# Five SBUF-only operations of the retention, moved from VectorE to GpSimd

## The chip, the cores and the metric

One core of a Trainium2 chip runs the whole program in one launch. The metric is the device time of that launch in microseconds (us). The engines are named as the profile names them: PE is TensorE, ACT is ScalarE, DVE is VectorE, POOL is GpSimd, SP is SyncE.

## The reference

The input x is 4 sequences of 512 tokens with 128 channels. Four sublayers follow one another, each with a residual:

```python
x = x + attn_a(_layernorm(x))      # chunked linear attention
x = x + ffn(_layernorm(x))         # six layers, see below
x = x + attn_b(_layernorm(x))      # the retention
x = x + ffn(_layernorm(x))         # the same six layers again
```

The six layers of `ffn` hold a local windowed attention (16 heads of 64, queries and keys normalised to length 1 and rotated) and a gated feed-forward. The retention, which the change touches, is:

```python
def _L0_attn_b_ref(X, W_Q, W_K, W_V):
    Q = xpos(X @ W_Q)                      # x * cos_s + rot * sin_s
    K = xpos(X @ W_K, downscale=True)
    V = X @ W_V
    D = decay_mask(L, GAMMA)
    ret = jnp.einsum('bnd,bmd->bnm', Q, K) * D[None]
    return ret @ V
```

## The kernel before

Channels lie on the 128 partitions, tokens on the free axis; a sequence is a tile of 128x512. After a first stage (the linear attention) the program is a pipeline of steps in which each engine runs its own list of instructions and waits on semaphores. Step s does the attention part of one sequence in one layer (`cur`) and, beside it, finishes the attention and does the feed-forward part of the sequence of step s-1 (`prev`). There are 48 such units of work, and they run through the two passes over the six layers without a break, so there are steps 0 to 48. Within a step the 16 heads go in four quads of four heads, g or k = 0 to 3.

The order on each engine is written by hand, in the function `step` of that engine. A quad goes through these operations:

- PE `project` makes queries and keys of a quad in PSUM. ACT `evacuate` writes their squares to `u` (L1093) and a scaled copy to `ab` (L1094).
- POOL `add_squares(k)` (L1287, twice 128x512) adds the squares of the two halves. It releases `sq_sum[0]` and `sq_sum[1]`.
- PE `norms(k)` (L806) sums them over the channels, once behind each of the two semaphores; each of the two fp32 matmuls stands in the trace as two passes, each with its weight load (PEld). ACT `inverse_norms` (L1105, L1107) turns them to inverse lengths.
- DVE `turn(k)` (L1342, twice) and `add_keys` (L1347), POOL `add_queries(k)` (L1291): the rotation, unnormalised. DVE `normalise_keys` (L1352, L1356) and POOL `normalise_queries(k)` (L1296) scale by the inverse length.
- SP sends the queries and keys to other partitions, PE `scores` (L827), DVE `less_maximum` (L1362, L1365), ACT exponentials (L1111), DVE `sums` (L1371, L1373) and `turn_weights` (L1377, L1380), PE `values` (L848).

At the end of a step DVE runs `second_residual` (L1411), which finishes the previous sequence's layer in `zT` and releases `x2`. The counter of `x2` starts four ahead, so that a wait for `now.count(x2, -2)` in step s is a wait for the `second_residual` of step s-1.

The retention has no steps of its own. It rides in steps 22 to 26, spread between the operations of the quads: its first half on one sequence (`ret1`) in steps 22 to 25, its second half (`ret2`) one step later, in steps 23 to 26. Those five steps are written out; steps 1 to 21 and most of those after 26 are loops. The order on PE at the start of a retention step is:

```python
                            project(0, (2, 3))
                            values(-3)
                            ret_keys_by_queries()
                            norms(0)
                            project(1, (0, 1))
                            ret_out()
                            scores(-1)
                            ret_mean()
```

`ret_keys_by_queries` (L927) waits for the sums `k_sum` and `q_sum` of the step before. On DVE the retention operations are, in order: `ret_decay` (L1454), `ret_add` (L1423), `ret_residual` (L1460), `ret_centre` (L1428), `ret_centre2` (L1465), `ret_norm` (L1433), `ret_part` four times (L1441), `ret_norm2` (L1470), and `ret_sum` twice (L1447). `ret_keys_by_queries` of step s feeds `ret_decay`, which is the first thing on DVE in step s, followed by `turn(0)`. POOL had in these steps the operations of the quads alone; PE banks in PSUM are taken in a fixed cycle of three, so PE also waits until DVE or ACT has read a bank (`bank_free`).

Of the kernel before, what the change touches and what calls it, by code (L numbers as in the profile page):

```python
# [3 lines left out]
def build_hybrid(nc, x_rows, tabs, wa, wb, wf, out):  # L4
# [10 lines left out]
    ALU, ACT, AX = mybir.AluOpType, mybir.ActivationFunctionType, mybir.AxisListType  # L15
# [14 lines left out]
    with ctx:  # L30
# [31 lines left out]
        xT = sb("xT", [C, TOK])  # L62
        zT = sb("zT", [C, TOK])
# [379 lines left out]
        def order_of(ret1, ret2):  # L443

            if not ret1 and not ret2:
# [16 lines left out]
        q_sum, k_sum = per_quad("q_sum"), per_quad("k_sum")  # L462
# [11 lines left out]
        x2 = Signal("x2", 1, 1, 4)  # L474
# [4 lines left out]
        R = {n: Signal("r_" + n) for n in ("x", "mean", "xc", "sq", "var", "lnv", "rstd", "xn", "k", "kr", "qr", "v", "q", "v_sb", "k_part", "kr_part",  # L479
                                           "qr_part", "q_part", "k_sum", "q_sum", "s0", "s1", "s2", "out", "x2", "mean2", "xc2", "sq2", "var2",  # L480
                                           "lnv2", "rstd2", "z", "sum")}
# [16 lines left out]
        def stage_ffn():  # L498
            scope = ExitStack()
            with scope:  # L500
# [27 lines left out]
                rc, rsq, rc2, rsq2, part, rvals = (t(n, [C, N]) for n in ("rc", "rsq", "rc2", "rsq2", "part", "rvals"))  # L528
                rqk = t("rqk", [C, 2, N])
# [24 lines left out]
                def columns(b):  # L554
                    return slice(N * b, N * b + N)
# [24 lines left out]
                def halves(s):  # L580

                    of = lambda first: s - first if isinstance(s, int) and 0 <= s - first < B else None
                    return of(RET1), of(RET2)
# [695 lines left out]
                @block.gpsimd  # L1279
                def _(pool):  # L1280
                    def step(s, prev, cur):
                        now = Steps(pool, s + 1, POOL_USES)

                        def add_squares(k):
                            for i in range(2):
                                pool.wait_ge(sq_done.sem, now.count(sq_done, 4 * k + 2 * i + 1))
                                nc.gpsimd.tensor_tensor(u[:, 2 * i + 1, :], u[:, 2 * i, :], u[:, 2 * i + 1, :], ALU.add).then_inc(sq_sum[i].sem, 1)  # L1287

                        def add_queries(k):
                            pool.wait_ge(turned.sem, now.count(turned, k))  # L1290
                            nc.gpsimd.tensor_tensor(w[:, 0:2, :], w[:, 0:2, :], ab[:, k % 2, 0:2, :], ALU.add).then_inc(q_sum.sem, 1)  # L1291

                        def normalise_queries(k):
                            pool.wait_ge(q_sum.sem, now.count(q_sum, k))
                            pool.wait_ge(gain.sem, now.count(gain, k))
                            nc.gpsimd.tensor_tensor(ab[:, k % 2, 0:2, :], w[:, 0:2, :], rn[:, 0:1, :].broadcast_to([128, 2, N]), ALU.mult).then_inc(rope_q.sem, 1)  # L1296

                        if halves(s) != (None, None):
                            for k in range(3):
                                add_squares(k)  # L1300
                                add_queries(k)
                                normalise_queries(k)
                            add_queries(3)
                            add_squares(3)
                            normalise_queries(3)
                        elif cur:
                            add_squares(0)
                            add_queries(0)
                            normalise_queries(0)
                            add_squares(1)  # L1310
                            add_squares(2)
                            add_queries(1)
                            normalise_queries(1)
                            add_queries(2)
                            normalise_queries(2)
                            add_queries(3)
                            add_squares(3)
                            normalise_queries(3)

                    nc.gpsimd.memset(kb[:, :, :], 0.0).then_inc(zeroed, 1)  # L1320
                    steps_of(pool, step)

                @block.vector
                def _(dve):
                    def step(s, prev, cur):
                        now = Steps(dve, s + 1, DVE_USES)
# [90 lines left out]
                                    nc.vector.tensor_scalar_mul(dst[:, 0:C:2], src[:, 1:C:2], -1.0).then_inc(r_turned, 1)  # L1417
                                    nc.vector.tensor_copy(dst[:, 1:C:2], src[:, 0:C:2]).then_inc(r_turned, 1)

                        def ret_add():  # L1420
                            if ret1 is not None:
                                dve.wait_ge(x2.sem, now.count(x2, -2))
                                nc.vector.tensor_tensor(xT[:, columns(ret1)], xT[:, columns(ret1)], zT[:, columns(ret1)], ALU.add).then_inc(R["x"].sem, 1)  # L1423

                        def ret_centre():
                            if ret1 is not None:
                                dve.wait_ge(R["mean"].sem, ret1 + 1)
                                nc.vector.tensor_tensor(rc[:, :], xT[:, columns(ret1)], f, ALU.subtract).then_inc(R["xc"].sem, 1)  # L1428

                        def ret_norm():  # L1430
                            if ret1 is not None:
                                dve.wait_ge(R["rstd"].sem, ret1 + 1)
                                nc.vector.tensor_tensor(rc[:, :], rc[:, :], rsq[:, :], ALU.mult).then_inc(R["xn"].sem, 1)  # L1433

                        def ret_part(name, to, tab):
                            if ret1 is not None:
# [2 lines left out]

                                    dve.wait_ge(R["k_sum"].sem, ret1 + 1)  # L1440
                                nc.vector.tensor_tensor(to, bank("ret", 0, name), tab[:, :], ALU.mult).then_inc(R[name + "_part"].sem, 1)  # L1441

                        def ret_sum(i, name, one, two):
                            if ret1 is not None:
                                dve.wait_ge(R[one + "_part"].sem, ret1 + 1)
                                dve.wait_ge(R[two + "_part"].sem, ret1 + 1)
                                nc.vector.tensor_tensor(rqk[:, i, :], rqk[:, i, :], part[:, :], ALU.add).then_inc(R[name].sem, 1)  # L1447

                        def ret_decay():
                            if ret2 is not None:  # L1450
# [13 lines left out]
                                dve.wait_ge(R["mean2"].sem, ret2 + 1)  # L1464
                                nc.vector.tensor_tensor(rc2[:, :], xT[:, columns(ret2)], bank("ret", 0, "mean2"), ALU.subtract).then_inc(R["xc2"].sem, 1)  # L1465

                        def ret_norm2():
                            if ret2 is not None:
                                dve.wait_ge(R["rstd2"].sem, ret2 + 1)
                                nc.vector.tensor_tensor(zT[:, columns(ret2)], rc2[:, :], rsq2[:, :], ALU.mult).then_inc(R["z"].sem, 1)  # L1470

                        if ret1 is not None or ret2 is not None:
                            ret_decay()
                            turn(0)
                            ret_add()
                            add_keys(0)
                            ret_residual()
                            normalise_keys(0)
                            ret_centre()
                            less_maximum(-1)  # L1480
                            ret_centre2()
                            sums(-1)
                            turn_weights(-1)
                            turn(1)
                            ret_norm()
                            add_keys(1)
                            ret_turn_weights()
                            normalise_keys(1)
                            less_maximum(0)
                            turn(2)  # L1490
                            sums(0)
                            ret_part("k", rqk[:, 1, :], kcos)
                            residual()
                            ret_norm2()
                            turn_weights(0)
                            ret_part("kr", part[:, :], ksin)
                            centred()
                            add_keys(2)
                            normalise_keys(2)
                            ret_part("qr", rqk[:, 0, :], qsin)  # L1500
                            less_maximum(1)
                            turn(3)
                            normed()
                            sums(1)
                            evacuate_out()
                            ret_sum(1, "k_sum", "k", "kr")
                            ret_part("q", part[:, :], qcos)
                            add_keys(3)
                            turn_weights(1)
                            next_low()  # L1510
                            for j in range(3):
                                gated(j)
                            ret_sum(0, "q_sum", "q", "qr")
                            less_maximum(2)
                            normalise_keys(3)
                            sums(2)
                            turn_weights(2)
                            second_residual()
                            return
# [147 lines left out]
```

## Time and profile before

| what | value |
|---|---|
| median of 3 runs | 3166.32 us (3164.66 to 3171.8) |
| time of the profiled execution | 3168.24 us |
| its span in the profile | 3166.5 us |
| PE busy | 3005.7 us, 95% |
| DVE busy | 2880.3 us, 91% |
| ACT busy | 2272.7 us, 72% |
| POOL busy | 1807.9 us, 57% |
| chain that ended last | PE 40%, DVE 23%, ACT 19%, issue 10% |

The profiled execution took 1.7 us more than its span, which is what lies around it, and it is 1.9 us above the median. The busy shares are means over 49 steps of which only five are touched; what bounds those five has to be read from their own stretch. A busy time of DVE or POOL holds time in which the instruction had been issued and was waiting for the other of the two engines, as the rows below show.

### The profile page before, as it was taken

To read this page: it belongs to the slowest core of one execution; us is meant where nothing else is said; L and a number is where in the kernel's file an instruction comes from. 1 tells how busy PE (TensorE), PEld (TensorE's weight loads), DVE (VectorE), ACT (ScalarE), POOL (GpSimd) and SP (SyncE) were. 2 spreads that over 40 slices of the span, in tenths; PEclk is the share of its full clock that TensorE was granted. 3 is DMA by queue.
4 is the path that set the end of the run, shared out by engine and by line. 5 is a ranking of instruction groups with operands and counts; after the bars stand their busy time and mean duration, and the time that the engine had idled before them with its cause. 6 is when DMAs were issued, how large, how long until landed. Compare 5 with 4: busy or idle time off the path is not lost.

```text
span 3166.5 us, 93664 instructions
## 1 busy us (share of the span) xinstructions
PE 3005.7 (95%) x37896; PEld 1857.5 (59%) x37896; DVE 2880.3 (91%) x2671; ACT 2272.7 (72%) x3707; POOL 1807.9 (57%) x823
## 2 busy tenths in 40 slices
PE   8699999999999999999999999999999999999996
PEld 4356555665665566565566656556656555665653
DVE  5599999999999999999999999999999999999995
ACT  4467777777777777776667777777777777777774
POOL 8556565555656555555445565555656565555652
PEclk9799999999999999999999999999999999999998
DMA  9544544543544544454344354454445445445542
GB/s 317 169 110 116 144 115 107 145 122 98 156 117 101 144 117 117 118 154 113 84 133 106 91 152 117 107 133 124 112 121 141 112 122 133 112 118 134 125 112 59
DMA packets 254405, 398.04 MB, mean 126 GB/s; under 512 B 51148, under 2 KB 84872, under 8 KB 254280
## 3 DMA queue, kind: packets, MB, share of 16 engines
q1 hardware_dynamic: 254280, 396.41, 47.8%
q8 instruction: 74, 1.21, 0.2%
q14 instruction: 51, 0.42, 0.0%
HBM read 64.64 MB, written 19.92 MB: 27 GB/s over the span
## 4 chain that ended last, share of the span: by engine, by line
PE 40%; DVE 23%; ACT 19%; issue 10%; SPq 1%; POOL 1%; DMA 1%; DVEq 0%; ACTq 0%; POOLq 0%
PE ps L848 6%; PE ps L806 5%; PE ps L866 5%; PE ps L882 5%; PE ps L827 5%; PE ps L787 4%; ACT f_ab L1094 4%; DVE f_mx L1362 4%; DVE f_p L1365 3%; ACT f_u L1093 3%; DVE f_p L1377 3%; ACT ps L1105 3%; PE ps L789 3%; PE ps L788 3%; ACT f_p L1111 3%
## 5 line engine op out<-in xcount | busy, mean ns | idle before, releaser
L1291 POOL TENSOR_TENSOR f_w<-f_w,f_ab 128x1024 f32<-128x1024 f32 x192 | 549.2, 2861 | 526.9 <-DVE f_w L1342 526.9
L1296 POOL TENSOR_TENSOR f_ab<-f_w,f_rn 128x1024 f32<-128x1024 f32 x192 | 594.1, 3094 | 390.9 <-DVE f_rn L1352 380.9
L1287 POOL TENSOR_TENSOR f_u<-f_u 128x512 f32<-128x512 f32 x384 | 589.1, 1549 | 365.3 <-ACT f_u L1093 359.8
L1094 ACT ACTIVATE f_ab<-ps,f_pa 128x512 f32<-128x512 f32 x768 | 542.1, 706 | 1.2
L1093 ACT ACTIVATE f_u<-ps 128x512 f32<-128x512 f32 x768 | 467.1, 608 | 99.3 <-PE ps L789 93.6
L1342 DVE TENSOR_TENSOR f_w<-f_ab,f_tan 128x1024 f32<-128x1024 f32 x384 | 500.4, 1343 | 4.1 <-POOL f_ab L1296 2.3
L848 PEld LDWEIGHTS ps<-f_tb,f_v 128*64 128x64 f32 x6144 | 396.0, 137 | 102.1 <-issue 78.5
L848 PE MATMUL ps<-f_tb,f_v 128*64 128x160 f32 (+1 forms) x6144 | 442.2, 297 | 11.9 <-DMA f_tb<-f_pt 10.7
L1105 ACT ACTIVATE ps<-ps 128x512 f32<-128x512 f32 x384 | 204.7, 574 | 340.7 <-PE ps L806 340.2
L787 PE MATMUL ps<-f_xh,f_wh 128*128 128x512 f32 x768 | 380.7, 496 | 54.8 <-ACT f_ab L1094 44.5
L806 PE MATMUL ps<-f_u,f_ones 128*128 128x512 f32 x768 | 370.2, 604 | 6.9 <-POOL f_u L1287 4.1
L866 PE MATMUL ps<-f_ot,f_wout 128*128 128x512 f32 x768 | 365.7, 599 | 2.8 <-DVE zT L1411 2.7
L827 PEld LDWEIGHTS ps<-f_kb,f_qb 64*32 64x32 f32 x24576 | 268.6, 105 | 107.3 <-issue 104.1
L1371 DVE TENSOR_REDUCE f_rs<-f_p 128x16 f32<-128x1024 f32 x192 | 233.4, 1216 | 102.5 <-ACT f_p L1111 102.5
L1356 DVE TENSOR_TENSOR f_ab<-f_w,f_rn 128x1024 f32<-128x1024 f32 x192 | 314.9, 1640 | 6.6
L1111 ACT ACTIVATE f_p<-f_p 128x1024 f32<-128x1024 f32 x192 | 202.7, 1056 | 147.6 <-DVE f_p L1365 147.4
L827 PE MATMUL ps<-f_kb,f_qb 64*32 64x64 f32 x24576 | 303.5, 226 | 2.2 <-issue 2.2
L789 PE MATMUL ps<-f_xh,f_wl 128*128 128x512 f32 x768 | 304.6, 397 | 0.0
L788 PE MATMUL ps<-f_xl,f_wh 128*128 128x512 f32 x768 | 302.3, 394 | 0.0
L1377 DVE TENSOR_TENSOR f_p<-f_p,f_rs 128x1024 f32<-128x1024 f32 x192 | 290.7, 1514 | 1.9
L882 PE MATMUL ps<-f_fq,f_w 128*128 128x512 f32 (+1 forms) x576 | 274.1, 611 | 11.3 <-issue 3.8
L1380 DVE STREAM_TRANSPOSE f_pt<-f_p 128x1024 f32<-128x1024 f32 x192 | 239.1, 1246 | 20.9
(165 smaller groups left out, 4822.9 us busy)
## 6 DMA issues: line engine op xcount, KB each, us to landing
f_kb<-f_ab SPq DMA_DIRECT2D x384, 256.0 KB, 3.6
f_qb<-f_ab SPq DMA_DIRECT2D x384, 256.0 KB, 3.6
f_tb<-f_pt SPq DMA_DIRECT2D x1344, 64.0 KB
f_wh<-split_w SPq DMA_DIRECT2D x48, 384.0 KB, 4.4
f_wl<-split_w SPq DMA_DIRECT2D x48, 384.0 KB, 4.2
a_w_raw<-wqkv SPq DMA_DIRECT2D x24, 384.0 KB, 4.6
split_w<-a_w_hi SPq DMA_DIRECT2D x24, 384.0 KB, 4.6
split_w<-a_w_lo SPq DMA_DIRECT2D x24, 384.0 KB, 5.5
```

The costliest lines, as they stand in the source:

```text
L787: nc.tensor.matmul(bank("qk", g, i), wh[:, g, i, :], xh[:, :], start=True, stop=False)
L806: last = nc.tensor.matmul(ps[:, NO[i], :], ones[:, :], u[:, 2 * i + 1, :], start=True, stop=True)
L827: last = nc.tensor.matmul(ps[rows, SS[h], c0:c0 + 64], qb[dims, pair, w0:w0 + WIN], kb[dims, pair, w0:w0 + 2 * WIN], start=False, stop=Tru ...
L848: last = nc.tensor.matmul(ps[rows, NO[pair], 128 * tile:128 * tile + WIN * windows], v[:, tile, d0:d0 + 64], tb[:, 0:windows, 8 * (h % 2) ...
L866: last = nc.tensor.matmul(f, wout[:, 2 * g + i, :], ot[:, 2 * g + i, :], start=g + i == 0, stop=g + i == QUADS)
L882: nc.tensor.matmul(bank(kind, -1, j)[0:m], w1[:, first + 128 * j:first + 128 * j + m], fq[:, :], start=True, stop=True).then_inc(ready.sem, 1)
L1093: nc.scalar.activation(u[:, i, :], bank("qk", g, i), ACT.Square).then_inc(sq_done.sem, 1)
L1094: nc.scalar.activation(ab[:, g % 2, i, :], bank("qk", g, i), ACT.Identity, scale=pa[:, g, i:i + 1]).then_inc(qk_read.sem, 1)
L1287: nc.gpsimd.tensor_tensor(u[:, 2 * i + 1, :], u[:, 2 * i, :], u[:, 2 * i + 1, :], ALU.add).then_inc(sq_sum[i].sem, 1)
L1291: nc.gpsimd.tensor_tensor(w[:, 0:2, :], w[:, 0:2, :], ab[:, k % 2, 0:2, :], ALU.add).then_inc(q_sum.sem, 1)
L1296: nc.gpsimd.tensor_tensor(ab[:, k % 2, 0:2, :], w[:, 0:2, :], rn[:, 0:1, :].broadcast_to([128, 2, N]), ALU.mult).then_inc(rope_q.sem, 1)
L1342: nc.vector.tensor_tensor(w[:, a:4:2, :], ab[:, k % 2, 1 - a:4:2, :], tan2[:, a:a + 1, :].broadcast_to([128, 2, N]), ALU.mult).then_inc(tu ...
```

## The change

Five operations of the retention whose operands all lie in SBUF leave the list of DVE and join that of POOL: `ret_add`, `ret_norm`, `ret_norm2` and the two `ret_sum`. Each keeps its operands, its shape (128x512, fp32) and the semaphores that it waits for and releases. `ret_add` now stands ahead of `add_squares(0)`, `ret_norm` behind `add_squares(1)`, `ret_norm2` behind `add_squares(2)`, the first `ret_sum` behind `normalise_queries(2)` and the second at the end of the step, behind `normalise_queries(3)`. In steps 22 to 25 `ret_add`, `ret_norm` and both `ret_sum` run, in steps 23 to 26 `ret_norm2`: 20 instructions in all.

```diff
@@ POOL, step @@
                         now = Steps(pool, s + 1, POOL_USES)
+                        ret1, ret2 = halves(s)
...
+                        def ret_add():
+                            if ret1 is not None:
+                                pool.wait_ge(x2.sem, now.count(x2, -2))
+                                nc.gpsimd.tensor_tensor(xT[:, columns(ret1)], xT[:, columns(ret1)], zT[:, columns(ret1)], ALU.add).then_inc(R["x"].sem, 1)
+
+                        def ret_norm():
+                            if ret1 is not None:
+                                pool.wait_ge(R["rstd"].sem, ret1 + 1)
+                                nc.gpsimd.tensor_tensor(rc[:, :], rc[:, :], rsq[:, :], ALU.mult).then_inc(R["xn"].sem, 1)
+
+                        def ret_sum(i, name, one, two):
+                            if ret1 is not None:
+                                pool.wait_ge(R[one + "_part"].sem, ret1 + 1)
+                                pool.wait_ge(R[two + "_part"].sem, ret1 + 1)
+                                nc.gpsimd.tensor_tensor(rqk[:, i, :], rqk[:, i, :], part[:, :], ALU.add).then_inc(R[name].sem, 1)
+
+                        def ret_norm2():
+                            if ret2 is not None:
+                                pool.wait_ge(R["rstd2"].sem, ret2 + 1)
+                                nc.gpsimd.tensor_tensor(zT[:, columns(ret2)], rc2[:, :], rsq2[:, :], ALU.mult).then_inc(R["z"].sem, 1)
+
                         if halves(s) != (None, None):
-                            for k in range(3):
-                                add_squares(k)
-                                add_queries(k)
-                                normalise_queries(k)
+                            ret_add()
+                            add_squares(0)
+                            add_queries(0)
+                            normalise_queries(0)
+                            add_squares(1)
+                            ret_norm()
+                            add_queries(1)
+                            normalise_queries(1)
+                            add_squares(2)
+                            ret_norm2()
+                            add_queries(2)
+                            normalise_queries(2)
+                            ret_sum(1, "k_sum", "k", "kr")
                             add_queries(3)
                             add_squares(3)
                             normalise_queries(3)
+                            ret_sum(0, "q_sum", "q", "qr")
@@ DVE, step: the four functions of the same names are taken out, and from its order @@
                             ret_decay()
                             turn(0)
-                            ret_add()
                             add_keys(0)
...
                             turn(1)
-                            ret_norm()
                             add_keys(1)
...
                             residual()
-                            ret_norm2()
                             turn_weights(0)
...
                             evacuate_out()
-                            ret_sum(1, "k_sum", "k", "kr")
                             ret_part("q", part[:, :], qcos)
...
                             for j in range(3):
                                 gated(j)
-                            ret_sum(0, "q_sum", "q", "qr")
                             less_maximum(2)
```

The order of POOL at the border of two retention steps, from quad 3 of step 23 into step 24. Before:

```order
123 L1291 TENSOR_TENSOR f_w<-f_w,f_ab 128x1024 [waits turned]
124 L1287 TENSOR_TENSOR f_u<-f_u 128x512 [waits sq_done] x2
125 L1296 TENSOR_TENSOR f_ab<-f_w,f_rn 128x1024 [waits gain,q_sum]
126 L1287 TENSOR_TENSOR f_u<-f_u 128x512 [waits sq_done] x2
127 L1291 TENSOR_TENSOR f_w<-f_w,f_ab 128x1024 [waits turned]
```

and in the changed kernel, where line 1302 is `ret_add`, 1313 is `ret_sum`, and 1288, 1292 and 1297 are what 1287, 1291 and 1296 were:

```order
131 L1292 TENSOR_TENSOR f_w<-f_w,f_ab 128x1024 [waits turned]
132 L1288 TENSOR_TENSOR f_u<-f_u 128x512 [waits sq_done] x2
133 L1297 TENSOR_TENSOR f_ab<-f_w,f_rn 128x1024 [waits gain,q_sum]
134 L1313 TENSOR_TENSOR f_rqk<-f_rqk,f_part 128x512 [waits r_qr_part,r_q_part]
135 L1302 TENSOR_TENSOR xT<-xT,zT 128x512 [waits x2]
136 L1288 TENSOR_TENSOR f_u<-f_u 128x512 [waits sq_done] x2
137 L1292 TENSOR_TENSOR f_w<-f_w,f_ab 128x1024 [waits turned]
```

Between `normalise_queries(3)` of one step and the squares of quad 0 of the next, where nothing stood, there are now two instructions, and the second waits for `x2`.

The order of DVE at the same border, before, from `second_residual` (L1411) and `ret_decay` (L1454) on:

```order
308 L1411 SCALAR_TENSOR_TENSOR zT<-ps,f_pf,f_x 128x512 [waits f_w2]
309 L1454 TENSOR_TENSOR f_hid<-ps,f_decay 128x512 [waits r_s0]
310 L1454 TENSOR_TENSOR f_hid<-ps,f_decay 128x384 [waits r_s1]
311 L1454 TENSOR_TENSOR f_hid<-ps,f_decay 128x128
312 L1454 TENSOR_TENSOR f_hid<-ps,f_decay 128x256 [waits r_s2]
313 L1342 TENSOR_TENSOR f_w<-f_ab,f_tan 128x2x512 [waits qk_read,rope_k,rope_q]
314 L1342 TENSOR_TENSOR f_w<-f_ab,f_tan 128x2x512
315 L1423 TENSOR_TENSOR xT<-xT,zT 128x512 [waits x2]
316 L1347 TENSOR_TENSOR f_w<-f_w,f_ab 128x1024 [waits turned]
317 L1460 TENSOR_TENSOR xT<-xT,ps 128x512 [waits r_out,r_x]
318 L1352 SCALAR_TENSOR_TENSOR f_rn<-ps,f_cos 128x1024 [waits n_inv]
```

and in the changed kernel, where 1443, 1470, 1374, 1379, 1476 and 1384 are the lines of 1411, 1454, 1342, 1347, 1460 and 1352:

```order
299 L1443 SCALAR_TENSOR_TENSOR zT<-ps,f_pf,f_x 128x512 [waits f_w2]
300 L1470 TENSOR_TENSOR f_hid<-ps,f_decay 128x512 [waits r_s0]
301 L1470 TENSOR_TENSOR f_hid<-ps,f_decay 128x384 [waits r_s1]
302 L1470 TENSOR_TENSOR f_hid<-ps,f_decay 128x128
303 L1470 TENSOR_TENSOR f_hid<-ps,f_decay 128x256 [waits r_s2]
304 L1374 TENSOR_TENSOR f_w<-f_ab,f_tan 128x2x512 [waits qk_read,rope_k,rope_q]
305 L1374 TENSOR_TENSOR f_w<-f_ab,f_tan 128x2x512
306 L1379 TENSOR_TENSOR f_w<-f_w,f_ab 128x1024 [waits turned]
307 L1476 TENSOR_TENSOR xT<-xT,ps 128x512 [waits r_out,r_x]
308 L1384 SCALAR_TENSOR_TENSOR f_rn<-ps,f_cos 128x1024 [waits n_inv]
```

The only row that left this place is `ret_add`; `turn(0)` is now followed by `add_keys(0)` directly.

## Rows read from the trace of the kernel before

**Rows 1.** Busy time by stretch: step 21, steps 22 and 23; column heads first
```profile
core 0: us, PE busy (x) PEld busy (x) DVE busy (x) ACT busy (x) POOL busy (x), PEclk, DMA share, GB/s
1410.00:1470.00 60.00, 56.23 (x768) 35.52 (x766) 54.84 (x53) 46.15 (x75) 35.02 (x15) 1.00 0.53 135
1470.00:1543.00 73.00, 69.23 (x805) 42.32 (x806) 70.48 (x71) 48.37 (x79) 37.30 (x18) 1.00 0.38 96
1543.00:1615.00 72.00, 70.91 (x816) 43.90 (x815) 70.69 (x70) 49.89 (x82) 36.02 (x16) 1.00 0.45 116
```

**Rows 2.** Groups of instructions by line, DVE: line, shapes, count, busy, mean ns
```profile
L1447 DVE TENSOR_TENSOR f_rqk<-f_rqk,f_part 128x512 f32<-128x512 f32 x8 | 9.7, 1210 | 0.0
...
L1423 DVE TENSOR_TENSOR xT<-xT,zT 128x512 f32<-128x512 f32 x4 | 2.7, 684 | 0.0
```

**Rows 3.** Chain of waits, end of step 23: start us, us, what
```profile
1601.98 1.73 PE ps L806 x4
...
1603.74 1.08 ACT ps L1105 x2
...
1605.88 1.24 DVE f_rn L1352
...
1609.82 1.89 DVE f_p L1377
...
1612.98 0.63 DVE zT L1411
```

**Rows 4.** Timeline, all engines, steps 23 to 24: start us, us, instruction
```profile
1607.25 3.36 POOL L1296 TENSOR_TENSOR f_ab<-f_w,f_rn 128x1024 f32<-128x1024 f32 x1 [10.49 <-DVE f_rn L1352]
...
1610.57 3.49 POOL L1287 TENSOR_TENSOR f_u<-f_u 128x512 f32<-128x512 f32 x2
...
1611.45 2.43 PE L927 MATMUL ps<-f_rqk 128*128 128x512 f32 x8
...
1613.53 1.67 DVE L1454 TENSOR_TENSOR f_hid<-ps,f_decay 128x512 f32<-128x512 f32 x4
1613.71 1.88 PE L806 MATMUL ps<-f_u,f_ones 128*128 128x512 f32 x4
...
1614.57 0.19 PEld L806 LDWEIGHTS ps<-f_u,f_ones 128*128 128x128 f32 x1 [0.20 <-issue]
...
1615.12 2.35 DVE L1342 TENSOR_TENSOR f_w<-f_ab,f_tan 128x1024 f32<-128x1024 f32 x2
```

**Rows 5.** Timeline of POOL, then of DVE, step 23
```profile
1571.26 3.49 POOL L1287 TENSOR_TENSOR f_u<-f_u 128x512 f32<-128x512 f32 x2
...
1563.31 3.38 DVE L1347 TENSOR_TENSOR f_w<-f_w,f_ab 128x1024 f32<-128x1024 f32 x1
...
1571.39 4.44 DVE L1342 TENSOR_TENSOR f_w<-f_ab,f_tan 128x1024 f32<-128x1024 f32 x2
```

**Rows 6.** Waits in step 22, last row step 23: us, times, longest
```profile
PE ps L909 <- DVE f_rqk L1441: 1.3, 1, 1.3
...
PE ps L882 <- DVE f_part L1441: 0.8, 1, 0.8
...
PE ps L909 <- DVE f_rqk L1441: 0.3, 1, 0.3
```

**Rows 7.** Timeline of POOL, DVE and PE, step 21 to 22
```profile
1467.86 3.47 POOL L1287 TENSOR_TENSOR f_u<-f_u 128x512 f32<-128x512 f32 x2
...
1466.98 0.66 DVE L1411 SCALAR_TENSOR_TENSOR zT<-ps,f_pf,f_x 128x512 f32 x1
...
1470.27 3.27 DVE L1342 TENSOR_TENSOR f_w<-f_ab,f_tan 128x1024 f32<-128x1024 f32 x2
...
1470.25 2.32 PE L806 MATMUL ps<-f_u,f_ones 128*128 128x512 f32 x4 [1.60 <-POOL f_u L1287]
```

**Rows 8.** Timeline of ACT, step 23: the two inverse deviations of the retention
```profile
1560.88 0.67 ACT L1165 ACTIVATE f_rsq<-f_rsq 128x512 f32<-128x512 f32 x1
...
1572.47 0.61 ACT L1185 ACTIVATE f_rsq<-f_rsq 128x512 f32<-128x512 f32 x1
```

More of the change, by code:

```diff
@@ L1418, in ret_turn_weights @@
                                     nc.vector.tensor_copy(dst[:, 1:C:2], src[:, 0:C:2]).then_inc(r_turned, 1)
[L1420 to L1423, printed above, removed]
                         def ret_centre():
@@ L1428, in ret_centre @@
                                 nc.vector.tensor_tensor(rc[:, :], xT[:, columns(ret1)], f, ALU.subtract).then_inc(R["xc"].sem, 1)
[L1430 to L1433, printed above, removed]
                         def ret_part(name, to, tab):
@@ L1441, in ret_part @@
                                 nc.vector.tensor_tensor(to, bank("ret", 0, name), tab[:, :], ALU.mult).then_inc(R[name + "_part"].sem, 1)
[L1443 to L1447, printed above, removed]
                         def ret_decay():
@@ L1465, in ret_centre2 @@
                                 nc.vector.tensor_tensor(rc2[:, :], xT[:, columns(ret2)], bank("ret", 0, "mean2"), ALU.subtract).then_inc(R["xc2"].sem, 1)
[L1467 to L1470, printed above, removed]
                         if ret1 is not None or ret2 is not None:
```

## The prediction

> **What bounds the kernel now.** Only steps 22 to 26 are touched, so I read busy time by stretch first. In step 21 PE is busy 56.2 of 60.0 us; in step 23 it is busy 70.9 of 72.0 and DVE 70.7, POOL only 36.0 [rows 1]. Both PE and DVE are full. The reader should see two different kinds of full. PE's time is matmuls back to back. DVE's holds waiting: `add_keys(1)` takes 3.38 us and the two halves of a turn 4.44 [rows 5], where the pair of L1342 takes 2.35 in an undisturbed place [rows 4]. These are instructions with two SBUF inputs, issued while a POOL instruction runs. So PE's own work, 72.0 - 70.9 = 1.1 us below the step's length, is the floor of a retention step, and what DVE gives up can bring back no more than PE's waits on DVE.
>
> Those waits come from the list of waits [rows 6]: 1.3 us (bank of `kr`) and 0.8 (bank of `q`) in step 22; in steps 23 to 25 the 0.8 is there again and the other is 0.3. Together 2.1 + 3 x 1.1 = 5.4 us.
>
> Then I read the chain of waits over the border of two steps, because the change puts two POOL instructions there. It runs from `norms(3)` on PE, done at 1603.71, over ACT's inverse lengths (from 1603.74), DVE's `normalise_keys(3)` (1605.88), `turn_weights(2)` (1609.82) to `second_residual`, which ends at 1612.98 + 0.63 = 1613.61 [rows 3]. Each of these starts within a few hundredths of its predecessor's end or behind a neighbour that itself hangs on `norms(3)`; DVE being less loaded earlier in the step doesn't shorten it.
>
> **What the change removes.** Four DVE instructions in step 22, five in steps 23 to 25, one in step 26. One costs 0.68 us by itself [rows 2]; the two sums average 1.21 [rows 2] since one of each pair waits behind POOL. That is 12 x 0.68 + 9.7 = 17.9 us. Also, with `ret_add` and `ret_norm` gone from between turn and `add_keys`, DVE issues `add_keys` directly behind the turn and should reach it before POOL's `add_queries` takes the pair of ports, so its 3.38 falls towards 1.2. I cost all of it at nothing beyond the 5.4 us above: what hides it is PE, full in these steps. I take the whole 5.4, because DVE gets ahead by five instructions of 0.68 us and up to twice 2.2 us of waiting in each step, and the waits are on DVE's place in its list; the bound below is none of it.
>
> Here the Trainium skill (Perfetto Trace Analysis, Optimizing Scalar/DVE Operations) says that work may be handed to GPSIMD when DVE is saturated, but that the two share a read port, so it might not help. By its first half alone the result would be the 5.4 us gained. The rows show what the second half means here, and more: the receiver stands on PE's path at one point.
>
> **What it adds on POOL.** The price of a 128x512 add there: the two squares at 1610.57 take 3.49 us. DVE's L1377, issued at 1609.82, gets the ports when `normalise_queries(3)` ends at 1607.25 + 3.36 = 1610.61 and holds them until 1611.71 [rows 3, 4]; the rest, 1614.06 - 1611.71 = 2.35, is two squares, 1.18 each. 20 of these are 24 us on an engine idle half of the time, so the total is free and each place counts.
>
> Three places are covered. `ret_norm` needs ACT's result of 1560.88 + 0.67 = 1561.55 [rows 8] and is done by about 1563.9 even behind a turn's half; `add_queries(1)` slips by some 1.5 us, and `normalise_queries(1)` waits for DVE's next gain anyway. `ret_norm2` needs 1572.47 + 0.61 = 1573.08 [rows 8], while the squares ahead of it run until 1571.26 + 3.49 = 1574.75 [rows 5]: no wait. The first `ret_sum` stands in a stretch in which POOL waits for `turn(3)`. If this cover were gone, each would cost its 1.18 us.
>
> The other two stand at the border. **Step 23 to 24**, with the times of before:
> - 1611.71: the second `ret_sum` starts, behind L1377; done at 1612.9. PE's `ret_keys_by_queries`, before at 1611.45 [rows 4], waits for it: 1.5 us late. Its last pass, and with it `ret_decay`, moves from 1615.20 to about 1615.7, and `turn(0)` from 1615.12 to 1615.7.
> - `ret_add` waits for `x2`: 1613.61, and 0.1 for the signal; 1613.7 to 1614.9. Behind it on POOL stand the squares of quad 0, which before began at 1610.57.
> - First square 1614.9 to 1616.1. DVE's first half of the turn has asked for the ports since 1615.7 and takes them next, 1.1 us, to 1617.2. Second square to 1618.4. That a waiting DVE instruction goes between two squares is seen at 1571.26: squares 3.49 and turn 4.44 together, each beside the other [rows 5]; 2 x 1.18 + 1.1 = 3.5.
> - PE's `norms(0)` needs the second square for its third pass, which before began at 1614.57 [rows 4], 0.5 us behind the square. Now 1618.45: **3.9 us** in which PE has nothing to do, since `norms(0)` heads its list.
>
> Bounds: if POOL's second square goes before DVE, 2.7; if both halves of the turn go before it, 5.0. I take 3.9, nearest to the row at 1571.26. It happens at three borders (22 to 23, 23 to 24, 24 to 25): 11.7 us.
>
> **Step 21 to 22** has no second sum, and `second_residual` comes early (1466.98 + 0.66 [rows 7]), so `ret_add` runs at once. The squares at 1467.86 end at 1471.33, and PE already waits 1.6 us for them [rows 7]. One add is 1.2 more, and the turn that asks at 1470.27 [rows 7], too late before to go between the squares, now does: 1.1 more. Together 2.3; lower bound 1.2.
>
> **Step 25 to 26** has the sum and no `ret_add`. `ret_keys_by_queries` waits 1.5 us; the squares end at 1612.9 + 2.4 = 1615.3, before the third pass of the delayed `norms(0)` at 1616.1. So 1.5.
>
> Sum: 11.7 + 2.3 + 1.5 - 5.4 = **+10.1 us**. The profiled execution, 3168.24, would be 3178.3; that execution is 1.9 above the median, so against the median 3166.32 it is 3176.4.
>
> **The rivals.**
> 1. DVE was the bound. For it: DVE is busy 70.7 of 72 [rows 1], and nearly every piece of the chain [rows 3] is DVE's. Against it: PE's 70.9. It decides if the squares of quad 0 still reach `norms(0)` in time, which takes a slack of 3.9 us where I read 0.5. Then only the recovered waits count: 3166.3 - 5.4 = 3160.9, not slower, and just inside what a measurement can tell; with DVE's relief felt in steps 22 and 26 too, at most some 11 us less.
> 2. POOL keeps the ports from one square to the next. The border costs 2.7 and the entry 1.2: 8.1 + 1.2 + 1.5 - 5.4 = +5.4, so 3171.7, hardly to be told from no change. Against it stands the row at 1571.26. The Trainium skill (SBUF — State Buffer, Who interferes with whom) has the ports go for a whole instruction to whichever of the two was issued first; by that rule the turn, waiting already, goes before a square issued later, and the trace agrees with the 4.44 us.
> 3. The relief brings back nothing and DVE takes both halves of the turn first: 3 x 5.0 + 2.3 + 1.5 = +18.8, so 3185.1. For it: PE's waits on a bank may hang on POOL's sums now, as the bank of `q` is read only after `k_sum`. Against: that sum is done some 4 us before PE's `q`.
> 4. The five operations don't do on POOL what I take. The order rows show them there; their shape and type are those of the squares. I fold this into case 3.
>
> **How the numbers follow.** About 0.2%, 6.3 us, is what a measurement of this kernel can tell from no change. The forecast gets 0.66, rival 1 0.12, rival 2 0.15, rivals 3 and 4 0.07. Within the forecast, 0.06 falls below +6.3 by noise of the runs (they spread over 7 us) and by the bounds. So slower: 0.60 + 0.07 + 0.03 of rival 2 = 0.70; faster: less than half of rival 1, 0.05; same: the rest, 0.25. The range runs from 3168, just short of rival 2 less the runs' noise, to 3183, short of rival 3.
>
> **What would show it.** In the profile after: PE waiting for POOL's L1288 ahead of `norms(0)`, 2 to 3 us before its first pass or its third, at the start of steps 22 to 25; POOL's L1302 idle before it until DVE's `second_residual`; PE or its weight load for `ret_keys_by_queries` waiting for L1313, about 1.5 us, in steps 23 to 26; no wait of 0.8 for the bank of `q`; DVE's busy time down by 20 us or more. Retention steps of some 75 us in place of 72 show it right. I am wrong if POOL's squares of quad 0 end before PE needs them, or if steps 23 to 25 get shorter.

## The result, and the profile after

| | before | after |
|---|---|---|
| median | 3166.57 us (12 runs, 3164.66 to 3173.67) | 3174.43 us (12 runs, 3169.71 to 3180.88) |
| ratio | | 1.0023, 95% interval 1.0015 to 1.0031 |
| profiled execution, time and span | 3168.24, 3166.5 us | 3173.41, 3171.6 us |
| PE, DVE, ACT, POOL busy | 3005.7, 2880.3, 2272.7, 1807.9 | 2961.9, 2871.1, 2273.9, 1848.0 |
| chain that ended last: PE, DVE, ACT, issue, POOL | 40, 23, 19, 10, 1% | 45, 19, 19, 10, 2% |

The kernel became slower, by 7.9 us in the medians. The spans of the two profiles differ by 5.1 only, because the steps ahead of the retention happened to run some 3 us shorter in the second. So this part uses one measure throughout, **the stretch**: from the start of `second_residual` in step 21 to its start in step 26. Before, it starts at 1466.98 [rows 7] and ends here (timeline of DVE, kernel before):

```profile
1823.79 0.71 DVE L1411 SCALAR_TENSOR_TENSOR zT<-ps,f_pf,f_x 128x512 f32<-128x512 f32 x1
```

That is 356.8 us. After, from the same view of the changed kernel:

```profile
1464.20 0.66 DVE L1443 SCALAR_TENSOR_TENSOR zT<-ps,f_pf,f_x 128x512 f32 x1
...
1828.91 0.71 DVE L1443 SCALAR_TENSOR_TENSOR zT<-ps,f_pf,f_x 128x512 f32<-128x512 f32 x1
```

That is 364.7 us, 7.9 more. The timeline of PE at the border of steps 23 and 24, changed kernel, for the PE rows of [rows 4]:

```profile
1602.56 1.88 PE L806 MATMUL ps<-f_u,f_ones 128*128 128x512 f32 x4
...
1613.66 2.40 PE L927 MATMUL ps<-f_rqk 128*128 128x512 f32 x8 [1.41 <-issue]
1617.07 1.10 PE L806 MATMUL ps<-f_u,f_ones 128*128 128x512 f32 x2 [1.01 <-POOL f_u L1288]
1619.27 1.10 PE L806 MATMUL ps<-f_u,f_ones 128*128 128x512 f32 x2 [1.11 <-POOL f_u L1288]
```

The first row is `norms(3)`. Behind it PE waits three times where before it did not wait: 1.41 us before `ret_keys_by_queries`, 1.01 before the first and 1.11 before the second half of `norms(0)`. The two other borders show the same figures to 0.01. POOL and DVE at that place, for [rows 3, 4], line 1297 being the old 1296, 1313 `ret_sum`, 1302 `ret_add`, 1288 the squares; 1409 the old 1377, 1443 `second_residual`, 1374 the turn, 1379 `add_keys`:

```profile
1607.99 3.36 POOL L1297 TENSOR_TENSOR f_ab<-f_w,f_rn 128x1024 f32<-128x1024 f32 x1 [10.02 <-DVE f_rn L1384]
1611.31 2.25 POOL L1313 TENSOR_TENSOR f_rqk<-f_rqk,f_part 128x512 f32<-128x512 f32 x1
1614.43 1.27 POOL L1302 TENSOR_TENSOR xT<-xT,zT 128x512 f32<-128x512 f32 x1 [0.86 <-DVE zT L1443]
1615.65 3.48 POOL L1288 TENSOR_TENSOR f_u<-f_u 128x512 f32<-128x512 f32 x2
```

```profile
1610.56 1.88 DVE L1409 TENSOR_TENSOR f_p<-f_p,f_rs 128x1024 f32<-128x1024 f32 x1
...
1613.64 0.71 DVE L1443 SCALAR_TENSOR_TENSOR zT<-ps,f_pf,f_x 128x512 f32<-128x512 f32 x1
...
1616.67 3.54 DVE L1374 TENSOR_TENSOR f_w<-f_ab,f_tan 128x1024 f32<-128x1024 f32 x2
1620.24 1.23 DVE L1379 TENSOR_TENSOR f_w<-f_w,f_ab 128x1024 f32<-128x1024 f32 x1
```

The reader should see four handovers. POOL's sum shows 2.25 us because DVE's L1409, issued earlier, takes the ports first. `ret_add` starts when `second_residual` ends, having waited 0.86. Only then come the squares; their 3.48 and the turn's 3.54 are one alternation. And `add_keys` of quad 0 takes 1.23, where it took 3.38 before. (That of quad 1, 3.38 before as well [rows 5], takes 2.20 in step 23.)

Busy time from the `second_residual` of step 22 to that of step 23, before and then after. The columns are those of [rows 1]; the bounds are the same events in both kernels, as the steps of the changed kernel lie at other times:

```profile
1540.91:1612.90 71.99, 70.90 (x815) 43.89 (x815) 70.69 (x71) 49.89 (x82) 36.02 (x17) 1.00 0.44 114
```

```profile
1538.44:1613.64 75.20, 70.42 (x809) 43.86 (x815) 68.61 (x66) 49.96 (x82) 46.01 (x21) 1.00 0.41 109
```

The step takes 75.2 us in place of 72.0. PE does the same work, 70.4 and 70.9 us busy, but now stands idle for 4.8 us where it was 1.1. DVE's busy time fell by 2.1 us in it.

### The profile page after: what moved, and what is told of

Same layout as the page of the kernel before. It is cut to its first block, busy times and chain, and to the rows that moved or that the text cites. A ratio compares the mean times of both kernels' runs of the same rounds, so it can differ in the third digit from the quotient of the medians.

```text
span 3171.6 us, 93426 instructions
## 1 busy us (share of the span) xinstructions
PE 2961.9 (93%) x37658; PEld 1854.2 (58%) x37896; DVE 2871.1 (91%) x2651; ACT 2273.9 (72%) x3707; POOL 1848.0 (58%) x843
## 4 chain that ended last, share of the span: by engine, by line
PE 45%; ACT 19%; DVE 19%; issue 10%; POOL 2%; SPq 1%; DMA 1%; DVEq 0%; ACTq 0%; POOLq 0%
PE ps L848 7%; PE ps L866 6%; PE ps L806 5%; PE ps L827 5%; PE ps L882 5%; PE ps L787 4%; ACT f_ab L1094 4%; ACT f_u L1093 3%; DVE f_mx L1394 3%; DVE f_p L1397 3%; PE ps L789 3%; PE ps L788 3%; ACT ps L1105 3%; DVE f_p L1409 3%; ACT f_p L1111 2%
## 5 line engine op out<-in xcount | busy, mean ns | idle before, releaser
L1288 POOL TENSOR_TENSOR f_u<-f_u 128x512 f32<-128x512 f32 x384 | 590.5, 1554 | 369.3 <-ACT f_u L1093 362.2
L1374 DVE TENSOR_TENSOR f_w<-f_ab,f_tan 128x1024 f32<-128x1024 f32 x384 | 506.9, 1360 | 6.7 <-ACT f_ab L1094 4.4
L848 PEld LDWEIGHTS ps<-f_tb,f_v 128*64 128x64 f32 x6144 | 396.2, 137 | 101.0 <-issue 76.1
L848 PE MATMUL ps<-f_tb,f_v 128*64 128x160 f32 (+1 forms) x6144 | 442.4, 297 | 11.3 <-DMA f_tb<-f_pt 9.3
L806 PE MATMUL ps<-f_u,f_ones 128*128 128x512 f32 x768 | 370.6, 603 | 15.8 <-POOL f_u L1288 13.4
L827 PEld LDWEIGHTS ps<-f_kb,f_qb 64*32 64x32 f32 x24576 | 267.7, 105 | 106.4 <-issue 103.6
L1388 DVE TENSOR_TENSOR f_ab<-f_w,f_rn 128x1024 f32<-128x1024 f32 x192 | 318.2, 1657 | 6.6
L827 PE MATMUL ps<-f_kb,f_qb 64*32 64x64 f32 x24576 | 302.3, 226 | 8.5 <-issue 1.7
L1409 DVE TENSOR_TENSOR f_p<-f_p,f_rs 128x1024 f32<-128x1024 f32 x192 | 298.7, 1556 | 1.9
```

What stands on the lines that cost most here:

```text
L806: last = nc.tensor.matmul(ps[:, NO[i], :], ones[:, :], u[:, 2 * i + 1, :], start=True, stop=True)
L827: last = nc.tensor.matmul(ps[rows, SS[h], c0:c0 + 64], qb[dims, pair, w0:w0 + WIN], kb[dims, pair, w0:w0 + 2 * WIN], start=False, stop=Tru ...
L848: last = nc.tensor.matmul(ps[rows, NO[pair], 128 * tile:128 * tile + WIN * windows], v[:, tile, d0:d0 + 64], tb[:, 0:windows, 8 * (h % 2) ...
L1374: nc.vector.tensor_tensor(w[:, a:4:2, :], ab[:, k % 2, 1 - a:4:2, :], tan2[:, a:a + 1, :].broadcast_to([128, 2, N]), ALU.mult).then_inc(tu ...
```

## The experiments

All changes of place below are to the changed kernel unless it says otherwise. The times are medians; the stretch is of one profile each.

| kernel | ratio to before (95%) | stretch, us |
|---|---|---|
| before | 1 | 356.8 |
| changed | 1.0023 (1.0015 to 1.0031) | 364.7 |
| e1, `ret_add` back on DVE | 0.9994 (0.9985 to 1.0003) | 357.0 |
| e2, second `ret_sum` back | 1.0030 (1.0016 to 1.0043) | 372.7 |
| e3, both back | 0.9984 (0.9975 to 0.9993) | 353.8 |
| e4, all on POOL, two reordered | 0.9974 (0.9963 to 0.9986) | 349.8 |
| e5, before with `ret_add` alone moved | 1.0058 (1.0042 to 1.0075) | 372.9 |
| e6, before, the five on one column | 0.9976 (0.9966 to 0.9986) | 350.1 |
| e7, e2 and a matmul in the wait | 1.0024 (1.0015 to 1.0034) | 362.5 |
| e8, e5 and a matmul in the wait | 1.0035 (1.0023 to 1.0048) | 365.7 |

**e1: `ret_add` back.**

```diff
 POOL:
-                            ret_add()
                             add_squares(0)
 DVE:
                             turn(0)
+                            ret_add()
                             add_keys(0)
```

> The changed kernel with one of the five, ret_add, back on VectorE behind turn(0); the other four stay on GpSimd. Measure: from the start of second_residual in step 21 to its start in step 26; 356.8 us in the kernel before, 364.7 in the changed one. My theory (GpSimd's list ahead of the squares of quad 0 holds PE's norms(0)): the sum is now alone ahead of the squares, so steps 23 to 26 each keep PE's 1.4 us before ret_keys_by_queries, and both waits before norms(0) (1.0 and 1.1) go; the entry to step 22 is back at 1.6. Stretch 356.8 + 4 x 1.4 - 6.4 = 356.0, at most 358 as VectorE gets ret_add and its wait for the ports back; time as before, 3166 to 3168. Rival (every operation on GpSimd costs its share, 7.9 / 20 = 0.4 us each, through the shared ports): four of 20 gone, 363.1.

Measured: stretch 357.0, no difference in time that can be told. PE's timeline at the border of steps 23 and 24:

```profile
1610.86 2.40 PE L927 MATMUL ps<-f_rqk 128*128 128x512 f32 x8 [1.40 <-issue]
1613.09 1.88 PE L806 MATMUL ps<-f_u,f_ones 128*128 128x512 f32 x4
```

The wait before L927 stays at 1.40, and both halves of `norms(0)` (L806) follow without one. The entry to step 22 is back at 1.61. The rival's 363.1 falls.

**e2: the second sum back.**

```diff
 POOL:
                             normalise_queries(3)
-                            ret_sum(0, "q_sum", "q", "qr")
 DVE:
                             for j in range(3):
                                 gated(j)
+                            ret_sum(0, "q_sum", "q", "qr")
```

> The changed kernel with the second ret_sum back on VectorE; ret_add stays at the head of GpSimd's list. My theory: ret_add waits for second_residual whether the sum stands ahead of it or not, so PE's norms(0) starts its third pass as late as in the changed kernel; the 1.4 us before ret_keys_by_queries goes but comes back as wait before norms(0), and only the border to step 26, which has no ret_add, gains 1.4. Stretch 363.3. Rival (the two waits of PE add up, so that the sum is worth 4 x 1.4 = 5.6): 359.1.

Measured: 372.7, 8 us longer than the changed kernel, though less was moved. The waits came as expected: none before L927, then 2.6 and 1.1 us, 3.7 together in place of 3.5, and nothing at the border to step 26. That part of the theory stands; the expected 363.3 does not. PE's timeline in step 23, and its busy time and granted clock (the 1.00 or less behind the five busy times) right after:

```profile
1542.61 1.10 PE L806 MATMUL ps<-f_u,f_ones 128*128 128x512 f32 x2 [2.59 <-POOL f_u L1288]
1544.81 2.05 PE L806 MATMUL ps<-f_u,f_ones 128*128 128x512 f32 x2 [1.11 <-POOL f_u L1288]
...
1547.08 0.63 PE L788 MATMUL ps<-f_xl,f_wh 128*128 128x512 f32 x1
```

```profile
1544.00:1554.00 10.00, 9.19 (x146) 6.00 (x147) 4.63 (x4) 4.22 (x7) 4.07 (x2) 0.67 0.07 15
```

A matmul of 512 columns takes 0.63 us where it takes 0.39 elsewhere, and the mean granted clock of those 10 us is 0.67: for part of them PE ran at 1.2 GHz, not 2.4. What it had done before was wait 2.6 us in one piece. e7 and e8 take this up.

**e3: both back.** The edits of e1 and e2 together; `ret_norm`, `ret_norm2` and the first `ret_sum` stay on POOL.

> Only ret_norm, ret_norm2 and the first ret_sum on GpSimd; ret_add and the second ret_sum on VectorE, as before. My theory: the three are covered, no border is held, and VectorE is relieved of 12 of the 20; stretch 352 to 355, below the 356.8 of before; time 3161 to 3165. Rival (each operation on GpSimd costs 0.4): 361.5.

Measured: 353.8, and faster than before. No border wait is left, and the three covered moves pay.

**e4: all five on POOL, in another order.**

```diff
-                            ret_add()
                             add_squares(0)
+                            ret_add()
...
                             add_squares(3)
+                            ret_sum(0, "q_sum", "q", "qr")
                             normalise_queries(3)
-                            ret_sum(0, "q_sum", "q", "qr")
```

> All five on GpSimd as in the changed kernel, two of them at other places: ret_add behind add_squares(0) and the second ret_sum between add_squares(3) and normalise_queries(3), where its inputs are there and GpSimd waits some 10 us. My theory: no wait before ret_keys_by_queries, norms(0) as in the kernel before (1.6 at the entry to step 22, none later), the relief of VectorE kept: stretch 356.8 - 6.4 = 350.4, time about 3160. Rival (it is the number of operations on GpSimd and the shared ports that cost, not the order): 364.7.

Measured: 349.8, and the fastest kernel that computes the reference: 0.9974. Timelines of POOL and PE at the border of steps 23 and 24:

```profile
1598.37 3.36 POOL L1297 TENSOR_TENSOR f_ab<-f_w,f_rn 128x1024 f32<-128x1024 f32 x1 [6.65 <-DVE f_rn L1384]
1601.70 3.48 POOL L1288 TENSOR_TENSOR f_u<-f_u 128x512 f32<-128x512 f32 x2
1605.14 1.27 POOL L1302 TENSOR_TENSOR xT<-xT,zT 128x512 f32<-128x512 f32 x1
```

```profile
1602.54 2.43 PE L927 MATMUL ps<-f_rqk 128*128 128x512 f32 x8
1604.81 1.88 PE L806 MATMUL ps<-f_u,f_ones 128*128 128x512 f32 x4
```

The squares (L1288) follow `normalise_queries(3)` at once, `ret_add` comes behind them without waiting, and PE's L927 and L806 stand without a wait. As many operations on POOL as in the changed kernel, and 15 us less: the order is what costs.

**e5: `ret_add` alone.** The kernel before, with only this move:

```diff
 POOL:
                         if halves(s) != (None, None):
+                            ret_add()
                             for k in range(3):
 DVE:
                             turn(0)
-                            ret_add()
                             add_keys(0)
```

> The kernel before with one part of the change alone: ret_add on GpSimd ahead of add_squares(0), the other four on VectorE. My theory: the whole delay of norms(0) is in this one move: entry to step 22 +2.3, three borders 3.5 each, step 26 nothing, less some 3 us for VectorE's four operations and the waits for the ports behind them. Stretch 356.8 + 2.3 + 10.6 - 3 = 366.7, so slower than the changed kernel, 364.7, with four operations moved in place of 20. Rival (0.4 us for each operation moved): 358.4.

Measured: 372.9, 8 us above the changed kernel with a fifth of its moves. Waits before `norms(0)` of 2.4 to 2.5 and 1.1 us at each border. The sign and the place are as expected, the size is 6 us more; the granted clock again reads below 1.00 behind each border.

**e6: relief without a load on POOL.** The five stay on DVE and take one column each, so this kernel leaves most of their work out. One of the four edited lines:

```diff
-nc.vector.tensor_tensor(rc[:, :], rc[:, :], rsq[:, :], ALU.mult)
+nc.vector.tensor_tensor(rc[:, 0:1], rc[:, 0:1], rsq[:, 0:1], ALU.mult)
```

> The kernel before, with the five operations left on VectorE and cut to one column each (the rest of their work is left out), so VectorE is relieved and GpSimd's list is as before. My theory: PE's own work is the floor of a retention step, and only its waits on VectorE come back: stretch 350 to 353. Rival (VectorE is the bound of the retention steps, and what it is relieved of comes off the time: 20 operations of 0.5 and the waits for ports): 340 or less.

Measured: 350.1. DVE gives up its work on all 20 and the stretch falls by 6.7 us, not by 16 or more. PE is busy 340.9 us of these 350.1, DVE 321.7: PE's work is the floor.

**e7 and e8: break the wait.** One more matmul at the head of `norms(0)`, in e2 and in e5:

```diff
+                            if g == 0 and ret1 is not None:
+                                pe.wait_ge(o_read[0].sem, now.count(o_read[0], g - 3))
+                                pe.wait_ge(R["x"].sem, ret1 + 1)
+                                nc.tensor.matmul(ps[:, NO[0], :], mean_w[:, :], xT[:, columns(ret1)], start=True, stop=True)
                             for i in range(2):
```

> e2 with one more fp32 matmul of 512 columns on TensorE at the head of norms(0) in steps 22 to 25, released by ret_add's semaphore (about 1.2 us into the wait of 2.6 us); it lies inside the wait, its result is written over by norms(0). In e2 the granted clock falls to 0.50 (1.2 GHz) behind each unbroken wait of 2.5 us and more, in the changed kernel, where as much waiting lies in pieces of 1.4, 1.0 and 1.1 us, it stays at 1.00 at the three borders. Theory A (it is the unbroken wait that lets the clock fall, and the clock that makes e2 longer than the changed kernel): clock 1.00 behind the borders, stretch back from 372.7 to 363 to 366. Theory B (something else in e2's order costs the 9 us, the lower clock is incidental): 370 or more.

> e5 with the same matmul at the head of norms(0) in steps 22 to 25. Theory A: clock 1.00 behind the borders and a stretch back from 372.9 to 366 to 368, which is what was expected of e5 without a change of clock. Theory B: 371 or more.

Measured: e7 362.5, e8 365.7; theory A in both, e7 by 0.5 and e8 by 0.3 us better than its lower end. PE's timeline in e7 in step 23 (L805 is the added matmul, L810 `norms(0)`), and the 10 us behind:

```profile
1535.28 1.10 PE L805 MATMUL ps<-xT,mean_w 128*128 128x512 f32 x2 [1.22 <-POOL xT L1306]
1536.50 1.10 PE L810 MATMUL ps<-f_u,f_ones 128*128 128x512 f32 x2
1538.70 1.10 PE L810 MATMUL ps<-f_u,f_ones 128*128 128x512 f32 x2 [1.11 <-POOL f_u L1292]
...
1539.86 0.39 PE L788 MATMUL ps<-f_xl,f_wh 128*128 128x512 f32 x1
```

```profile
1537.00:1547.00 10.00, 8.75 (x153) 5.71 (x153) 7.40 (x7) 4.22 (x7) 6.55 (x3) 1.00 0.12 28
```

PE waits 1.22, runs the added matmul for 1.10, goes on with `norms(0)` and waits 1.11. Its matmul of 512 columns takes 0.39 again and the clock reads 1.00. With more work on PE the stretch is 10.3 us shorter than e2's, and 7.2 shorter in e8 than in e5. Over the stretch PE is busy 352.9 us in e2 and 345.4 in e7, so most of that difference is the same matmuls taking less time. The granted clock fell behind all eight border and entry waits of e2 and e5, and behind none of the eight of e7 and e8.

How far this shows in the whole time is less sure. The stretches come from one execution each, and e2's was the slowest of its five (3184.66), e7's the fastest of its ten (3166.44). Outside the stretch, where the retention's order was not touched, the ten profiles differ by up to 11 us. Against the kernel before, timed beside each, e2 is 10.3 us slower and e7 6.9, e5 15.1 and e8 13.0, and within each pair the intervals of the ratios overlap. The low clock itself is no accident of the profiled executions: averaged over a whole execution the granted clock was 0.986 to 0.988 in all nine runs of e2 and e5, mean 0.987, and 0.988 to 0.992 in the sixteen of e7 and e8, mean 0.990, as in the kernel before.

## Why the prediction was right

The forecast was 3176.4, the measured median is 3174.43; slower was given 0.7. By the steps of the working:

- **Where PE is held.** Right at every border, and shown: e1 takes one instruction away and both waits before `norms(0)` go, e4 leaves all 20 on POOL and all border waits go. The order of POOL's list is what costs, not the number of its operations. The shared ports add to it only through that order: DVE's half of a turn now goes between the two squares while PE waits, the 1.11 us in front of the second half of `norms(0)`.
- **The three borders, 3.9 us each.** From the end of the last pass of `norms(3)` to the third pass of `norms(0)` it was 1614.57 - 1603.71 = 10.9 us [rows 3, 4]. After, `norms(3)` starts at 1602.56 and takes 1.88, so it ends at 1604.44, and the third pass starts at 1619.27: 14.8, so 3.9 to 4.0 more. As rows of waiting it is 1.41 + 1.01 + 1.11 = 3.5. The sign that was named, 2 to 3 us before the first or the third pass, came as 1.0 and 1.1. Rival 2 (POOL keeps the ports between two squares) is out: squares 3.48, turn 3.54. The Trainium skill (SBUF — State Buffer, Who interferes with whom) has the ports go to whichever was issued first; the trace agrees, in the sum's 2.25 us behind L1409 as well.
- **The entry, 2.3 us.** Right for the wait: 2.81 + 1.11 less the 1.60 of before is 2.3. But the whole cost of the entry was 3.7, since the lower clock behind that wait was not in the sum. From the start of `values` (L848) to the mask of `scores` (L817), before and then after, it is 7.42 and 11.13 us:

```profile
1466.37 2.29 PE L848 MATMUL ps<-f_tb,f_v 128*64 128x160 f32 x32
...
1473.79 0.39 PE L817 MATMUL ps<-f_mask,f_identb 128*128 128x512 bf16 x1
```

```profile
1463.58 2.29 PE L848 MATMUL ps<-f_tb,f_v 128*64 128x160 f32 x32
1468.68 1.10 PE L806 MATMUL ps<-f_u,f_ones 128*128 128x512 f32 x2 [2.81 <-POOL f_u L1288]
1470.89 2.04 PE L806 MATMUL ps<-f_u,f_ones 128*128 128x512 f32 x2 [1.11 <-POOL f_u L1288]
...
1474.71 0.39 PE L817 MATMUL ps<-f_mask,f_identb 128*128 128x512 bf16 x1
```

- **The border to step 26, 1.5 us**: 1.40.
- **What comes back, 5.4 us.** This term was mis-sized. 7.9 = 3 x 3.95 + 3.7 + 1.4 - x gives x = 9.1. Of the waits on DVE that I had counted, 1.34 before the `kr` bank in step 22 did not go and the other 4.1 did; so did 0.59 and 0.29 before L848 in step 22, which I had not counted. These rows make 5.0. The other 4 us of x stand in no row of waiting that I can name and stay open. e4 and e6, which add no wait at a border, took 7.0 and 6.7 off the stretch. (Gaps of 0.35 and 0.78 us before L827 in the kernel before, and 0.99 in the changed one, are no such waits: they lie among the 128 matmuls of `scores`, where the program waits for nothing.)
- **The size.** +10.1 was forecast and +7.9 measured. The relief, 3.7 us larger than taken, and the lower clock at the entry, 1.4 us that nothing in the sum stood for, go against each other. That the forecast came within 2.2 us is in part luck.
- **DVE's busy time down by 20 us or more.** Wrong: 9.2. Groups of DVE before and after (busy us, mean ns):

```profile
L1342 DVE TENSOR_TENSOR f_w<-f_ab,f_tan 128x1024 f32<-128x1024 f32 x384 | 500.4, 1343 | 4.1 <-POOL f_ab L1296 2.3 <-ACT f_ab L1094 1.8
...
L1377 DVE TENSOR_TENSOR f_p<-f_p,f_rs 128x1024 f32<-128x1024 f32 x192 | 290.7, 1514 | 1.9
L1347 DVE TENSOR_TENSOR f_w<-f_w,f_ab 128x1024 f32<-128x1024 f32 x192 | 252.3, 1314 | 3.1
```

```profile
L1374 DVE TENSOR_TENSOR f_w<-f_ab,f_tan 128x1024 f32<-128x1024 f32 x384 | 506.9, 1360 | 6.7 <-ACT f_ab L1094 4.4 <-POOL f_ab L1297 2.3
...
L1409 DVE TENSOR_TENSOR f_p<-f_p,f_rs 128x1024 f32<-128x1024 f32 x192 | 298.7, 1556 | 1.9
L1379 DVE TENSOR_TENSOR f_w<-f_w,f_ab 128x1024 f32<-128x1024 f32 x192 | 239.6, 1248 | 3.3
```

`add_keys` gave back 12.7 us as argued, besides the 17.9 us removed, but the turns took 6.5 and L1409 8.0 more, and L1388 (L1356 before) 3.3. L1409 is seen above taking the ports ahead of the added sum; that all of the growth is waiting for POOL is argued from that place, not shown at each. By such groups DVE has 12.7 us less; the busy time, in which overlapping instructions count once, fell by the 9.2. It mattered little, as PE waited for DVE in one of the counted places only, the 1.34 of step 22.
- **Rival 1 (DVE is the bound).** Its mechanism is out by e6; the gain that it named, 5.4 us, is about what e4 reaches once nothing is ahead of the squares: 7.0 in the stretch, 7.9 in the medians.

## What to carry to other kernels

Before an operation goes to a less busy engine, look at what follows it there: the engine runs in order, and a sum and an add of 1.2 us each, the add waiting for a late signal, held the squares behind them, and with them a full TensorE, for 3.9 us at each of three borders. The same five moves gave 1.0023 or 0.9974 depending on two places in the list. Place a moved operation behind the one that the bound engine waits for, and at a point where its own inputs are long there.

## What was not expected of the hardware

The granted clock of TensorE depends on how the waiting is spread. In the changed kernel 3.5 us of waiting lie at a border in pieces of 1.41, 1.01 and 1.11, and the clock reads 1.00 behind them; at the entry to step 22, behind an unbroken 2.81 and another 1.11, it reads 0.66. Busy times and clock of the changed kernel:

```profile
1470.00:1475.00 5.00, 4.11 (x9) 2.31 (x9) 3.04 (x2) 2.00 (x4) 3.84 (x2) 0.66 0.34 79
1543.00:1553.00 10.00, 8.78 (x153) 6.09 (x155) 7.37 (x7) 4.68 (x8) 6.53 (x3) 1.00 0.09 22
```

In e2 (2.6 and 1.1) and e5 (2.5 and 1.1) it falls at the borders too; with a matmul of 1.10 us inside the same wait, in e7 and e8, it doesn't. PE lost about as much to waiting at a border in e2 as in the changed kernel, 3.7 and 3.5 us, and e2's stretch was 8.0 us longer. That is the opposite of what I expected from counting waits, though in the whole times the intervals of the two, 1.0016 to 1.0043 and 1.0015 to 1.0031, overlap.

How the waiting is spread is not all of it. Behind `second_residual` of step 26, PE waits 2.04 to 2.08 us for it in all ten profiles, in one piece, and the clock stayed at 1.00 in seven of them and fell in three, those of e2, e6 and e8. In the changed kernel it also read 0.66 from 1425 to 1430, in step 21, behind a single wait of 1.69. So the same wait can bring the lower clock in one execution and not in another; what decides it there is open. The twelve timed executions of the changed kernel have a mean clock of 0.987 to 0.990, on average a little under the 0.990 of its profile, so in some of them it may have fallen at more places than in the profile shown here.
